# The end of a two-layer kernel: last-stage row sums divided anew among TensorE, VectorE, ScalarE and GpSimd

## The reference

```python
scores = jax.nn.softmax(t @ gate_w.T, axis=-1)
weights, indices = jax.lax.top_k(scores, TOP_K)          # TOP_K = 2 of 16 experts
y = jnp.zeros_like(t)
for e in range(N_EXPERTS):
    w_e = jnp.sum(jnp.where(indices == e, weights, 0.0), axis=-1)
    y = y + _swiglu(t, w1[e], w3[e], w2[e]) * w_e[:, None]
z = _swiglu(t, sw1, sw3, sw2)                             # shared expert
out = x + _layernorm(y + z)
```

## Time and profile before

| | us |
|---|---|
| median of three timed runs | 681.43 |
| profiled execution, whole time | 684.4 |
| its span, first to last instruction | 682.6 |
| busy: PE, DVE, ACT, POOL | 608.7, 527.3, 517.4, 427.4 |
| last scatter issued by GpSimd (L1229) | 648.33 |
| eight loads of routed rows issued | 650.83 to 654.9 |
| stores issued | 668.82 to 679.7 |

### The profile page before, as it was taken

The page is one execution under the profiler, slowest core; times in us unless marked ns, Lnnn a source line. Parts: engine busy times, 40 slices in busy tenths (PEclk is TensorE's granted clock), DMA queues, the critical chain, the costliest instruction groups (busy, mean ns, idle before and its releaser), DMA issues.

```text
span 682.6 us, 12684 instructions
## 1 busy us (share of the span) xinstructions
PE 608.7 (89%) x4476; PEld 498.8 (73%) x4479; DVE 527.3 (77%) x899; ACT 517.4 (76%) x1182; POOL 427.4 (63%) x261
## 2 busy tenths in 40 slices
PE   5799999999994698899999999899998787879993
PEld 3388999999993445799999999887774443445662
DVE  6898999999997899899999999878534543444464
ACT  3999999999995988999999999865454442333435
POOL 0028999999997004799999999920224465455402
PEclk8979999999996999999999999999999988898997
DMA  7022333333320000344444444461111122122163
GB/s 191 6 64 82 111 112 112 111 103 111 111 82 1 1 4 21 103 153 153 155 148 150 152 154 154 137 202 61 56 48 61 63 73 83 63 77 64 54 262 123
DMA packets 41595, 67.76 MB, mean 99 GB/s; under 512 B 6688, under 2 KB 20928, under 8 KB 41536
## 3 DMA queue, kind: packets, MB, share of 16 engines
q1 hardware_dynamic: 37696, 56.50, 25.7%
q0 software_dynamic: 3840, 10.49, 4.8%
HBM read 57.28 MB, written 9.70 MB: 98 GB/s over the span
## 4 chain that ended last, share of the span: by engine, by line
ACT 44%; PE 24%; DVE 12%; POOL 11%; issue 3%; another core or an unknown queue 2%; DMA 2%; DVEq 1%; POOLq 0%; ACTq 0%; SPq 0%
ACT rings L1045 20%; POOL arena L1184 9%; PE both L1476 8%; ACT rings L1033 8%; ACT late L1033 8%; PE bank L1483 4%; PE both L1463 4%; DVE st L443 1%; POOL residual L1194 1%; ACT tok_a L923 1%; ACT rings L923 1%; PE bank L1584 1%; ACT tok_a L996 1%; DVE rings L866 1%
## 5 line engine op out<-in xcount | busy, mean ns | idle before, releaser
L1184 POOL TENSOR_TENSOR arena<-arena,rings 128x1024 f32<-128x1024 f32 x126 | 296.3, 2372 | 13.3 <-DVE arena L658 8.7
L1383 PE MATMUL both<-rings,tok_a 128*128 128x128 f32 x1152 | 171.7, 278 | 3.7 <-DVE arena L658 2.9
L1383 PEld LDWEIGHTS both<-rings,tok_a 128*128 128x128 f32 x1152 | 148.6, 191 | 7.8 <-ACT rings L1045 3.6
L658 DVE TENSOR_TENSOR_SCAN arena<-rings,both 128x1024 f32<-128x1024 f32 x64 | 143.7, 2275 | 9.4 <-ACT rings L1033 6.4
L658 DVE TENSOR_TENSOR_SCAN arena<-late,both 128x1024 f32<-128x1024 f32 x62 | 139.3, 2274 | 8.2 <-ACT late L1033 6.5
L1412 PE MATMUL bank<-ident,arena 128*128 128x128 f32 x1024 | 133.0, 273 | 3.5 <-POOL arena L1184 2.3
L1412 PEld LDWEIGHTS bank<-ident,arena 128*128 128x128 f32 x1024 | 115.6, 141 | 4.6 <-POOL arena L1184 2.7
L1045 ACT ACTIVATE rings<-tok_a,b_tok 128x256 f32<-128x256 f32 x224 | 104.3, 515 | 0.0
L1045 ACT ACTIVATE rings<-ident,b_tok 128x128 f32<-128x128 f32 x288 | 99.1, 408 | 0.3
L1385 PE MATMUL both<-ident,rings 128*128 128x128 f32 x448 | 90.7, 273 | 0.0
L1476 PE MATMUL both<-w_sb,rings 128*64 x160 | 59.5, 521 | 18.1 <-DVE rings L804 16.4
(11 more groups left out here) (233 smaller groups left out, 1073.1 us busy)
## 6 DMA issues: line engine op xcount, KB each, us to landing
rings<-c_rows SPq DMA_DIRECT2D x128, 256.0 KB, 3.3
w_sb<-w SPq DMA_DIRECT2D x18, 352.0 KB, 4.1
arena<-w SPq DMA_DIRECT2D x2, 2048.0 KB, 12.6
residual<-x SPq DMA_DIRECT2D x4, 512.0 KB, 5.7
x_rows<-tok_a SPq DMA_DIRECT2D x4, 512.0 KB, 2.6
tok_a<-y_tok SPq DMA_DIRECT2D x4, 512.0 KB, 6.5
w_sb<-y_tok SPq DMA_DIRECT2D x4, 512.0 KB, 7.2
out<-residual SPq DMA_DIRECT2D x8, 256.0 KB, 2.6
```

Of the source, the lines that this page charges most:

```text
L658: dve.tensor_tensor_scan(h_s, decay_s.rearrange("p h t -> p (h t)"), both[s % B_RING][:, :], 0.0, ALU.mult, ALU.add).then_inc(h_ready, 1)
L1184: pool.tensor_tensor(h_both, h_both, c_row, ALU.mult).then_inc(hc_ready, 1)
L1383: pe.matmul(o, tok_a[:, c, h * P:(h + 1) * P], v_ring[:, s % V_RING, j, 0:P], start=True, stop=True)
```

## The change

The change is in the last stage alone. Quarter 2 leaves TensorE: `mixed_first` is 3, `shared_part` is gone, and VectorE adds quarter 2's routed rows as it did quarter 1's. Quarter 1's go to two engines: ScalarE multiplies the loaded rows by their weights in place (`weighted`), and GpSimd adds them to `f_moe`, two chunks per instruction. The quarters are normed in the order 0, 2, 1, 3. VectorE and ScalarE now have a list each.

```diff
-        combine = [("gates", 1), ("gates", 2), ("m_add0", 0), ("gates", 3), ("m_add1", 0), ("m_add0", 1), ("gates", 4), ("m_add1", 1),
...
-        mixed_first = 2
+        combine = [("gates", 1), ("gates", 2), ("gates", 3), ("m_add0", 0), ("m_add1", 0), ("gates", 4), ("m_stat", 0), ("m_add0", 2),
...
+        combine_act = [("m_stat", 0), ("m_norm", 0), ("m_stat", 2), ("m_norm", 2), ("m_stat", 1), ("m_norm", 1), ("m_stat", 3),
+                       ("m_stat", 4), ("m_norm", 3), ("m_norm", 4)]
+        mixed_first = 3
...
+        def normed_before(c):
+
+            return {0: c, 1: c + CQ, 2: c - CQ, 3: c}[c // CQ]
...
                     if k:
-                        dve.wait_ge(rows_added, CQ * (2 * q + 1))
+                        dve.wait_ge(rows_added, CQ * (q + 1))
...
+                    elif q == 1:
+                        dve.wait_ge(rows_pooled, CQ)
                     else:
-                        dve.wait_ge(rows_added, 2 * CQ * (q + 1))
+                        dve.wait_ge(rows_added, CQ * (q + 2))
...
-                        dve.wait_ge(m_normed, c + 2)
+                        dve.wait_ge(m_normed, normed_before(c) + 2)
...
+            def weighted(k):
+
+                act.wait_ge(y_loaded[k][1], 16)
+                for c in range(CQ, 2 * CQ):
+                    act.activation(y_k[k][:, c, :], y_k[k][:, c, :], ACT.Copy, scale=weights[:, c, k:k + 1]).then_inc(rows_weighted, 1)
...
+                        if c == C - 1:
+                            act.preload_act_table_set("natural_log_exp_and_others")
+                            weighted(0)
                         if c == C:
-                            act.preload_act_table_set("natural_log_exp_and_others")
+                            weighted(1)
...
+            pool.wait_ge(moe_copied, 2 * CQ)
+            for k in range(2):
+                for c in range(CQ, 2 * CQ, 2):
+                    pool.wait_ge(rows_weighted, CQ * k + c + 2 - CQ)
+                    if k:
+                        pool.wait_ge(rows_pooled, c // 2 - 1)
+                    pool.tensor_tensor(f_moe[:, c:c + 2, :], f_moe[:, c:c + 2, :], y_k[k][:, c:c + 2, :], ALU.add)\
+                        .then_inc(rows_pooled, 1)
             for c in range(0, 2 * CQ, 2):
-                pool.wait_ge(m_normed, c + 2)
+                pool.wait_ge(m_normed, normed_before(c) + 2)
...
-                    if hi == C and c == lo:
-                        shared_part(2)
...
-            def shared_part(q):
-
-                for c in range(mix_part[q].start, mix_part[q].stop):
-                    pe.matmul(mix(c), ident[:, :], f_moe[:, c, :], start=c % 2 == 0, stop=False, skip_group_check=True)
```

More of the change, by code:

```diff
@@ L249, in sandwich_kernel @@
         y_loaded = [[sem(f"y_loaded{k}{q}") for q in range(Q)] for k in range(2)]
-        rows_added = sem("rows_added")
+        rows_added, rows_weighted, rows_pooled = sem("rows_added"), sem("rows_weighted"), sem("rows_pooled")
         weights_ready, mix_ready, mixed = sem("weights_ready"), sem("mix_ready"), sem("mixed")
@@ L299, in sandwich_kernel @@
         pool_last = [("y_add", 0), ("y_add", 1), ("y_add", 2), ("y_add", 3)]
-        combine = [("gates", 1), ("gates", 2), ("m_add0", 0), ("gates", 3), ("m_add1", 0), ("m_add0", 1), ("gates", 4), ("m_add1", 1),
-                   ("m_stat", 0), ("m_stat", 1), ("m_norm", 0), ("m_norm", 1), ("m_stat", 2), ("m_norm", 2), ("m_stat", 3),
-                   ("m_norm", 3), ("m_stat", 4), ("m_norm", 4), ("m_out", 2), ("m_out", 3), ("m_out", 4)]
-        mixed_first = 2
+        combine = [("gates", 1), ("gates", 2), ("gates", 3), ("m_add0", 0), ("m_add1", 0), ("gates", 4), ("m_stat", 0), ("m_add0", 2),
+                   ("m_add1", 2), ("m_stat", 2), ("m_norm", 0), ("m_norm", 2), ("m_stat", 1), ("m_norm", 1), ("m_stat", 3),
+                   ("m_stat", 4), ("m_out", 2), ("m_norm", 3), ("m_norm", 4), ("m_out", 3), ("m_out", 4)]
+        combine_act = [("m_stat", 0), ("m_norm", 0), ("m_stat", 2), ("m_norm", 2), ("m_stat", 1), ("m_norm", 1), ("m_stat", 3),
+                       ("m_stat", 4), ("m_norm", 3), ("m_norm", 4)]
+        mixed_first = 3
         mix_part = [slice(0, CQ), slice(CQ, 2 * CQ), slice(2 * CQ, 3 * CQ), slice(3 * CQ, 3 * CQ + 2), slice(3 * CQ + 2, C)]
+        def normed_before(c):
+            return {0: c, 1: c + CQ, 2: c - CQ, 3: c}[c // CQ]
         def expert_rows_out():
@@ L1162, in _ @@
             shared(SHARED_FIRST, C)
-            for name, q in combine[1:]:
+            for name, q in combine_act:
                 stage(name, q, 2)
```

## The result

The changed kernel takes 687.88 us in the median of six timed runs (685.98 to 690.36), the kernel before 681.77 (680.50 to 684.25) beside it. The ratio is 1.0083, with a 95% interval of 1.0054 to 1.0112: slower by 3.7 to 7.6 us. Forecast were 684.4 us, +3.0, with a range up to 686.0.

What follows compares the result with a forecast made beforehand. Bound by VectorE's adds, ScalarE's norms, VectorE's output adds, then the store queue; first norm 3.5 us later and stores less heaped move the end from 682.6 to 685.6, +3.0. Median 681.4 + 3.0 = 684.4 us, range 678.3 to 686.0.

Steps and rivals of the forecast that it cites:

- The sign: Whole kernel: slower by 3.0 us; chance of measurably slower 0.25, of the same 0.62, of faster 0.13.
- the mechanism for the largest term: Quarter 2's adds: VectorE and GpSimd alternate on their shared SBUF way, 7.7 us in place of 3.2; first norm 3.5 later.
- its rule for who gets in: Shared SBUF way: GpSimd gets in behind any VectorE instruction that fetches its scalar by a pointer, as at L549; forecast chance 0.50.
- Adds of quarter 2: VectorE's adds begin at 660.46, alternate with GpSimd's four until 668.05; first norm at 670.0.
- First three norms: ScalarE's norms of quarters 0, 2, 1: start at 670.0, quarter 2's ends at 675.55, quarter 1's starts at 676.3.
- Outputs of quarter 2: VectorE's output adds wait for GpSimd's first add of quarter 1 (677.3 to 678.5), then end at 679.75; last shifts follow.
- gets in everywhere: Rival: GpSimd gets in at every VectorE boundary, output adds too; end +3.8 us, 685.2; chance 0.10.
- The stores: End of kernel: stores issued from 679.2 to 682.65, queue full, 0.9 + 4.6 + 0.9 behind the first, end 685.6.
- up to the last scatter nothing is touched: Before the last stage: no change up to the last scatter, and the eight loads can't be issued earlier; worth nothing.
- The block holds: Rival: VectorE's adds keep GpSimd out but for one slip between blocks; first norm 667.35, 681.8 us; chance 0.22.
- No hindrance: Rival: VectorE and GpSimd adds don't slow each other; first norm 665.5, end -2.8 us, 678.6; chance 0.18.
- the rows taken off TensorE: TensorE: quarter 2's 16 routed rows go, but it ends near 667 and quarter 3 is needed 9 us later; nothing.

Runs made afterwards that it cites:

- k1_sliver: Changed kernel with GpSimd's four row adds of quarter 1 cut to 8 of 256 columns: ratio to the kernel before 1.0012, tail 32.5 us.
- k2_later: Changed kernel with GpSimd's row adds of quarter 1 held until VectorE has made all adds of quarter 2: ratio to the kernel before 1.0028, tail 33.2 us.
- m1_port: Separate small kernel: three GpSimd 128x512 adds against six VectorE instructions, six kinds, either engine ahead; each GpSimd add costs VectorE 1.0 to 1.1 us.
- k3_second: Changed kernel with GpSimd's row adds held until VectorE has made its first add of quarter 2: ratio to the kernel before 1.0100, tail 36.4 us.
- p4_tensor2: Changed kernel with quarter 2 back on TensorE, quarters normed and stored in order, quarter 1 still on ScalarE and GpSimd: ratio to the kernel before 0.9972.
- p8_order: Kernel before, same division of work, with gates, adds, norms, roots, outputs and stores reordered: 677.99 us beside 682.38, ratio 0.9932.

## Why the prediction was wrong

The sign was right, and the mechanism for the largest term; its rule for who gets in was wrong, and the size was short. In the profile, relative to the first add (forecast / measured):

- **Adds of quarter 2.** They begin 5.64 / 5.73 behind it, and GpSimd 5.8 / 5.5 behind it. GpSimd's last row add ends 11.7 / 11.0 and the first norm starts 15.2 / 15.0 behind it. The first norm is right to 0.2 us, GpSimd's end was 0.7 too late. This is the term that makes most of the loss: k1_sliver took it away alone and gave back 3.8 of 4.5, k2_later 3.1.
- **First three norms.** From the first to the second 3.6 / 3.7, to the third 6.3 / 6.4. The shift of quarter 2 met GpSimd's residual adds as forecast (1.14).
- **Outputs of quarter 2: the step that failed.** The prediction let them wait for one GpSimd add and run on, since they have no pointer scalar. They took turns with both: 2.88. The last norms came 9.95 / 11.2 behind the first, the last output 12.6 / 13.9. That is +1.2, and k4_outputs showed it: with GpSimd's partner adds cut down to 8 columns the two took 1.28 and the tail was 1.6 shorter. This is the place named by the rival "gets in everywhere", to which I gave 0.10.
- **The stores.** End behind the last output 3.0 / 3.6. The last byte moved at 682.65 by the windows, 2.0 behind the last output, which is what the forecast had. The rest lies between the last byte and the span's end, 0.9 us before the change and 1.5 here. It goes with the chip, as the table of the experiments shows, and the chips of these two profiles are not on record. So this 0.6 can't be put down to the change.

Together: 3.0 forecast, +1.2 at the outputs, +0.6 behind the last byte, -0.3 at loads and adds, is 4.5. By the medians it is 6.1 (687.88 - 681.77), 1.6 more. The interval is 3.7 to 7.6, so both lie in it. The 3.5 us between 684.4 and 687.88 are 1.5 in the tail, 0.3 by which the median of before came out higher with six runs, and 1.6 outside the tail.

Part of this 1.6 is real. Over the seven timed kernels with the changed division the ratio lies on average 1.1 us above what the tail gives, over the four others 0.2. The profiles show where some of it lies: from the last scatter's issue to the first load's issue it is 2.85 to 3.29 us in those seven, and 2.48 to 2.50 in the kernel before and the four others. Both groups ran on chips 4 and 15, so it is the kernel and not the chip. In the two main profiles it is 0.4 (2.50 and 2.90). The prediction had put this at nothing ("up to the last scatter nothing is touched, and the eight loads can't be issued earlier"): they were issued later. What of the change delays them is open, and so is the other 1.2.

So the failed step at the outputs does not by itself explain why the time left the range: 684.4 + 1.2 is 685.6, and the range went to 686.0. In all the miss is 1.2 at the outputs, 0.4 ahead of the first load, -0.3 at loads and adds, and 2.1 that no step of the kernel accounts for: 0.6 behind the last byte, 0.3 in the median of before, 1.2 open. The range left 0.8 us above its slowest rival for such things, while six executions of each kernel gave an interval of almost 4 us.

**Why the step failed.** I took the one row with a pointer (L549) as the difference between a block that lets GpSimd in and one that doesn't. That gave the right size for quarter 2's adds and a wrong rule. m1_port shows no difference by pointer: 1.1 us per GpSimd add for L71 without one, 1.0 for L73 with one. The trace of the kernel before could have told, since at 264.03 L534, without a pointer, let GpSimd in. Given turns at each boundary, the outputs must pay too. The Trainium skill, "SBUF — State Buffer", section "Who interferes with whom", says that whoever issues first gets the lock and the other blocks. m1_port, k3_second and the rows of the changed kernel shown above agree; the two rows at 257 and 271 us do not, and I had let them outweigh it. Two rows of eight of the same line, from another part of the kernel, decided a chance of 0.10 that should have been the largest.

**The rivals.** "The block holds" fell with k3_second. "No hindrance" fell with the first profile. "Everywhere" had the mechanism right: it forecast +3.8 for the tail, 0.7 too little, and since it took 0.9 behind the last byte in both kernels, +3.8 to the last byte too, where +3.8 to +3.9 was measured.

**What TensorE gave.** The prediction valued the rows taken off TensorE at nothing. No run tested that alone. p4_tensor2, which gives quarter 2 back to TensorE together with other edits, came out faster, but how much of it is TensorE's it does not show.

## What to carry to other kernels

A GpSimd operation on 128x512 in SBUF is not free beside VectorE: here each one put VectorE back by 1.0 to 1.1 us, whatever the form of VectorE's instruction in the runs that tried it, unless VectorE was idle or in statistics. Before giving GpSimd work at a kernel's end, lay its adds beside VectorE's row and count the turns; a tiny instruction that others wait for (a 128x4 shift) pays as much as a large one. If three engines and a store queue follow one another, try the order first: p8_order gained 0.7% with no work moved between engines. And when a stage ends in a queue of stores, ask which add the queue stands behind: here it was quarter 2's, not the last.

## What the hardware showed unexpectedly

- The two engines take turns one instruction each, and neither a pointer scalar nor a head start changed it (m1_port: 6.90 and 6.60 us with VectorE or GpSimd ahead). Even a `TENSOR_SCALAR` from SBUF to SBUF, which reads one tile, pays: 1.49 us instead of 0.41 (L75).
- A VectorE shift of 128x4 values that takes 0.13 us took 1.14, the rest of the GpSimd add in front of it.
- Between the last byte stored and the end of the span lay 0.8 to 0.9 us in five profiles and 1.4 to 1.8 in seven. Where the chip is on record, the short ones are all of chip 4 and the long ones of chips 11, 14 and 15.
- At 257 and 271 us of the kernel before GpSimd was kept out for 3.6 us, which no rebuilt stretch reproduced, and which the same line did not show in its six other executions.
